# Two cross-attention blocks on one core: fp16 parts for the projections of x and context, a buffer for the gate, another head and another order

## The reference

```
block 0 (8 heads of 40):
  hs   = attention(x Wq, enc Wk, enc Wv)        enc = context[:, :124]   (FIRST)
  q1   = ca^T Wq_ca, 128 of its 192 rows        ca  = context[:, 124:]   (4 tokens)
  hs1  = attention(q1, x, x)                                             (CA)
  hs2  = attention(hs1 Wq, ca Wk_ca, ca Wv_ca)
  x    = (hs + hs2) Wout + b_out + x
block 1 (20 heads of 16):
  h = ln1(x); x = attention(h q1, h k1, h v1) o1_w + o1_b + x            (SELF)
  h = ln2(x); x = attention(h q2, context k2, context v2) o2_w + o2_b + x  (CROSS)
  h = ln3(x); a, g = split(h ff_w1 + ff_b1); x = (a * gelu(g)) ff_w2 + ff_b2 + x
```

## Time and profile before

| what | value |
|---|---|
| runs | 3941.24, 3950.0, 3958.27 us, median 3950.0 |
| profiled execution | 3965.49 us, its span 3963.6 us |
| granted TensorE clock, mean | 0.966 |
| PE / PEld / DVE / ACT / POOL busy | 90% / 72% / 58% / 57% / 50% |

### The profile page before, as it was taken

The page is one execution under the profiler, slowest core; times in us unless marked ns, Lnnn a source line. Parts: engine busy times, 40 slices in busy tenths (PEclk is TensorE's granted clock), DMA queues, the critical chain, the costliest instruction groups (busy, mean ns, idle before and its releaser), DMA issues.

```text
span 3963.6 us, 112057 instructions
## 1 busy us (share of the span) xinstructions
PE 3580.9 (90%) x38314; PEld 2867.6 (72%) x38314; DVE 2308.9 (58%) x5535; ACT 2268.7 (57%) x4084; POOL 1966.4 (50%) x2229
## 2 busy tenths in 40 slices
PE   6499999999999999999999999999999999999999
PEld 5377777777777777777777777777777777777777
DVE  6466556556555655655556556555655656556555
ACT  2356655665556556556655665566566556655664
POOL 0345444554555445555554554545445555554553
PEclk9799999999999999999999999999999999999999
DMA  4332333222233332232333322233332232333321
GB/s 138 63 61 53 58 61 66 59 46 60 59 55 61 67 61 49 53 65 51 63 63 66 59 46 60 56 58 61 67 64 47 53 64 53 63 63 66 59 46 42
DMA packets 417600, 238.71 MB, mean 60 GB/s; under 512 B 44315, under 2 KB 416715, under 8 KB 416843
## 3 DMA queue, kind: packets, MB, share of 16 engines
q1 hardware_dynamic: 405317, 229.62, 29.6%
q10 hardware_dynamic: 11910, 3.04, 0.3%
HBM read 153.50 MB, written 79.06 MB: 59 GB/s over the span
## 4 chain that ended last, share of the span: by engine, by line
PE 36%; issue 30%; POOL 17%; DVE 5%; SPq 4%; DMA 3%; ACT 3%; POOLq 1%; ACTq 0%; DVEq 0%
PE bank L1412 35%; POOL PT L519 10%; DMA xin<-in_x 3%; DVE mx L1025 2%; ACT PT L742 2%; POOL cQ L526 2%; POOL XA L496 1%; POOL cK L526 1%; SPq L365 1%; POOL rstd L566 1%; SPq L363 1%; POOL XB L496 1%; PE bank L1446 1%; PE bank L1531 1%; SPq L361 1%
## 5 line engine op out<-in xcount | busy, mean ns | idle before, releaser
L519 POOL TENSOR_TENSOR PT<-P,PT 128x512 f16<-128x512 f32 (+1 forms) x924 | 1068.8, 1157 | 642.1 <-ACT PT L742 640.8
L1412 PE MATMUL bank<-hT,w_ff_w 128*128 128x256 f16 x5440 | 651.6, 277 | 1.7 <-DVE hT L1054 1.7
L1025 DVE TENSOR_REDUCE mx<-bank 128x4 f32<-128x512 f32 (+1 forms) x924 | 579.6, 680 | 104.4 <-PE bank L1412 96.5
L1412 PEld LDWEIGHTS bank<-hT,w_ff_w 128*128 128x128 f16 x5440 | 532.5, 100 | 73.2 <-issue 6.5
L1412 PE MATMUL bank<-mxs,pick 84*128 84x128 f16 (+1 forms) x3696 | 513.4, 220 | 0.0
L1412 PE MATMUL bank<-w_ff,F 128*128 128x320 f32 x1360 | 411.5, 442 | 1.3 <-DVE F L1104 1.3
L1412 PEld LDWEIGHTS bank<-mxs,pick 84*128 84x128 f16 (+1 forms) x3696 | 375.1, 103 | 16.8 <-issue 8.2
L1412 PEld LDWEIGHTS bank<-V,PT 128*128 128x128 f16 (+1 forms) x9504 | 314.5, 96 | 84.0 <-POOL PT L519 37.9
L723 ACT ACTIVATE P<-bank,ff_b,scale 128x256 f32<-128x256 f32 x340 | 187.8, 562 | 324.9 <-PE bank L1412 285.4
L1412 PE MATMUL bank<-Qs,Ks 96*128 96x128 f16 x2640 | 361.7, 220 | 0.1
L1412 PE MATMUL bank<-V,PT 128*128 128x17 f16 (+1 forms) x9504 | 343.7, 172 | 17.1 <-POOL PT L519 14.3
(11 more groups left out here) (274 smaller groups left out, 7295.4 us busy)
## 6 DMA issues: line engine op xcount, KB each, us to landing
Ks<-scratch_k SPq DMA_DIRECT2D x198, 160.0 KB, 4.5
Qs<-scratch_q SPq DMA_DIRECT2D x198, 160.0 KB, 5.7
scratch_k<-cK SPq DMA_DIRECT2D x134, 128.0 KB, 1.8
scratch_q<-cQ SPq DMA_DIRECT2D x134, 128.0 KB, 2.1
Q0s<-scratch_q SPq DMA_DIRECT2D x99, 160.0 KB
K0s<-scratch_k SPq DMA_DIRECT2D x99, 160.0 KB
cT<-in_cT SPq DMA_DIRECT2D x136, 96.0 KB, 2.0
xin<-in_x SPq DMA_DIRECT2D x34, 320.0 KB, 3.2
```

The source lines that it names most:

```text
L519: nc.gpsimd.tensor_tensor(PT[0:keys, n % PT_SLOTS, 1, :], P[0:keys, n % P_SLOTS, :], PT[0:keys, n % PT_SLOTS, 0, :], ALU.subtract).then_in ...
L1025: nc.vector.tensor_reduce(mx[:, g % 2, 4 * u:4 * u + 4], bank[:, :].rearrange("p (h s) -> p h s", h=4)[:, :, 0:keys], axis=AX.X, op=ALU.ma ...
L1412: return nc.tensor.matmul(o, lhsT, rhs, start=start, stop=stop)
```

## The change

Inputs x and context are scaled by a power of two and split into fp16 parts once a step (`split_x` and `split_context` on ACT, three activations each; `low_x` and `low_context` on POOL), and `Wq`, `Wk`, `Wv`, `k2`, `v2` become fp16 parts in the head. `Q0T` is then 8 fp16 matmuls a chunk and `K0T`, `K2T`, `V0`, `V2` are 5 each. `gate` becomes a tile of its own, and the waits between `gelu` and `exps` go. The high and low chunks use `fixed` factors. `V2` and `K2T` read the same context parts as `V0` and `K0T`, so `cT2` and its loads go. `load_next` comes right after `stack_self` on SP and waits for `vca` and for the context's low part. The order of all engines is another one: `ff0` to `ff3` stand among the first scores, `ff4` to `ff9` as before between SELF and CROSS; `K0T0` to `K0T2` come together early; `K2T0`, `K2T1` and `V0_1` before CROSS. In the head the products of the tokens come first, in four parts with a store each, the shifts are spread beside the splitting, the reduces take the absolute value in one pass, and POOL does most of the clearing.

```diff
+MATSX, MATSK = ("Wq",), ("Wk", "Wv", "k2", "v2")
+MATS16 = MATSN + MATSX + MATSK
+PASSES_C = ((1, 0, 0), (3, 0, 0), (1, 1, 0), (2, 0, 1), (2, 1, 1))
+PASSES_X = ((1, 0, 0), (1, 1, 0), (4, 0, 0), (2, 0, 1), (2, 1, 1), (5, 0, 1), (3, 0, 2), (3, 1, 2))
...
-    Q0T0 XT0_0 Q0T1 XT0_1 Q0T2 K1T0 K1T1 K1T2 Q1T0 Q1T1 Q1T2 S0 S1 V0_0 V1_0 mx0 S2 S3 T0 K0T0 T1
-    V1_1 mx1 K0T1 T2 S4 S5 S6 S7 S8 T3 vca mx2 S9 S10 T4 S11 S12 T5 S13 caT0 T6 mx3 T7 T8 caT1 K0T2
-    T9 T10 T11 T12 T13 V0_1 outT1_0 ff0 ff1 outM1_0 outT1_1 ff2 ff3 outM1_1 XT1_0 ff4 s4 XT1_1 ff5
-    Q2T0 Q2T1 Q2T2 ff6 ff7 mT ff8 mB ff9 S14 S15 S16 S17 y1 S18 S19 mx4 S20 S21 S22 T14 S23 K2T0 T15
...
+    Q0T0 XT0_0 XT0_1 S0 Q0T1 Q0T2 K1T0 K1T1 K1T2 Q1T0 Q1T1 Q1T2 S1 ff0 S2 S3 ff1 ff2 mx0 K0T0 ff3 T0
+    V1_0 K0T1 mx1 K0T2 V0_0 T1 V1_1 T2 S4 S5 S6 S7 S8 T3 vca mx2 S9 T4 S10 T5 S11 T6 S12 S13 caT0
+    mx3 T7 T8 T9 T10 T11 T12 T13 caT1 ff4 outT1_0 ff5 ff6 ff7 outT1_1 outM1_0 outM1_1 ff8 XT1_0 ff9
+    XT1_1 s4 Q2T0 Q2T1 Q2T2 mT mB V0_1 K2T0 K2T1 y1 S14 S15 S16 S17 S18 mx4 S19 S20 T14 S21 T15 S22
...
-        gate = P[:, 0, :].rearrange("p (t n) -> p t n", t=2)
+        gate = sb("gate", [128, 2, GS])
...
             def load_next(i):
-                sp.wait_ge(v_done, v_job(i, LOOP_JOBS, "V0_1"))
+                sp.wait_ge(v_done, v_job(i, LOOP_JOBS, "vca"))
+                sp.wait_ge(c16_ready, i + 1)
...
+            def low_x(i):
+                pool.wait_ge(x_high, i + 2)
+                nc.gpsimd.tensor_tensor(x16[:, 3:6, :], xT[:, :, :], x16[:, 0:3, :], ALU.subtract).then_inc(x16_ready, 1)
+            def low_context(i):
+                pool.wait_ge(c_high, i + 1)
+                nc.gpsimd.tensor_tensor(c16[:, 2:4, :], cT[:, :, :], c16[:, 0:2, :], ALU.subtract).then_inc(c16_ready, 1)
...
+            def split_x(i):
+                act.wait_ge(step_loaded, i * LOADS_STEP + 2 * LOADS_STEP)
+                act.wait_ge(next_ready, i + 2)
+                act.wait_ge(j_full, done(i, LOOP_JOBS.number("Q0T2"), "J"))
+                nc.scalar.activation(xT[:, :, :], xT[:, :, :], ACT.Copy, scale=next_factor[:, SX:SX + 1])\
+                    .then_inc(x_scaled, 1)
+                act.wait_ge(x_scaled, i + 2)
+                nc.scalar.activation(x16[:, 0, :], xT[:, 0, :], ACT.Copy, scale=lower[:, :])
+                nc.scalar.activation(x16[:, 1:3, :], xT[:, 1:3, :], ACT.Copy).then_inc(x_high, 1)
...
-                elif t == 0:
-                    act.wait_ge(low_p, units_done(min(i, STEPS) if isinstance(i, int) else i, LAST_UNIT[SELF, 1]))
+                else:
+                    act.wait_ge(v_done, v_job(i - 1, LOOP_JOBS, f"ff{FFT + t - 2}"))
...
-                if n == LAST_UNIT[SELF, 1] + 1:
-                    act.wait_ge(v_done, v_job(i, LOOP_JOBS, f"ff{FFT - 1}"))
...
-            def chunk(i, name, c, wn, rows_k, src, at, rows):
-                if name == "K2T":
-                    pe.wait_ge(step_loaded, i * LOADS_STEP + 2 * LOADS_STEP)
+            def chunk(i, name, c, wn, src, passes, at, rows):
+                if c == 0:
+                    pe.wait_ge(x16_ready if src is x16 else c16_ready, i + 1)
                 bank = j_next(i, LOOP_JOBS, f"{name}{c}")
-                transposed(bank, wn, rows_k, src, at[c], rows[c]).then_inc(j_full, 1)
+                transposed16(bank[0:rows[c], 0:GS], wn, src, at[c], rows[c], passes).then_inc(j_full, 1)
...
             pe.wait_ge(tokens_loaded, TOKENS)
...
+            row_shifts_of(1, "q1")
             pe.wait_ge(kca_copied, 1)
+            products(0)
+            products(1)
+            row_shifts_of(0, "k1")
+            row_shifts_of(3, "v1")
+            products(2)
+            row_shifts_of(2, "q2").then_inc(row_shifts, 1)
+            products(3)
...
+            ff_shifts(0, 6)
...
             extremes_turned(-1, HEAD_JOBS)
+            ff_shifts(6, 13)
             extremes_everywhere(-1, HEAD_JOBS, QUANTITIES)
+            ff_shifts(13, 2 * FFT).then_inc(shifts_ready, 1)
```

More of the change, by code:

```diff
@@ L583, in _ @@
             token_queries(-1)
+            low_x(-1)
             assert links[0] == POOL_HEAD_LINKS
@@ L1173, in _ @@
                                         None, ALU.mult)
-            for m, n in enumerate(MATSN):
+            link(-1, nc.vector.memset(amax[:, :, :], 0.0))
+            dve.wait_ge(kca_ready, 1)
+            for c, r in enumerate(CH0):
+                for h in range(HC0[c]):
+                    last = nc.vector.tensor_scalar(
+                        kca[c][0:r, :, h, :], j_bank[c + 2][0:r, 0:B * T4].rearrange("p (b t) -> p b t", t=T4),
+                        mask0[0:r, h:h + 1], None, ALU.mult)
@@ new lines, in _, with lows @@
+            link(-1, last)
+            link(-1, nc.vector.tensor_scalar(qk_b[:, :], qk_b[:, :], scale[:, 2:3], None, ALU.mult))
+            extremes(128, 9, qk_b[:, :], AX.X)
+            dve.wait_ge(scale_ready, 1)
+            highs = [0]
+            def lows(names):
+                for n in names:
+                    for k in range(BLOCKS[n]):
+                        highs[0] += 1
+                        dve.wait_ge(high_ready, highs[0])
+                        last = nc.vector.scalar_tensor_tensor(out=w16[n][:, 1, k, :], in0=raw[n][:, k, :],
+                                                              scalar=gains[:, NORM_OF[n], k:k + 1], in1=w16[n][:, 0, k, :],
+                                                              op0=ALU.mult, op1=ALU.subtract)
+                return last
@@ L1469, in chunk16, with values @@
                 transposed16(bank[0:CH1[c], 0:GS], wn, hTn, AT1[c], CH1[c]).then_inc(j_full, 1)
-            def values(i, name, b, wn, src):
+            def values(i, name, b, wn):
+                if b == 0:
+                    pe.wait_ge(c16_ready, i + 1)
                 bank = j_next(i, LOOP_JOBS, f"{name}_{b}")
-                for k, rk in enumerate(CHC):
-                    last = mm(bank[:, 0:H], src[0:rk, k, b * S:(b + 1) * S], w[wn][0:rk, k, :], k == 0, k == 1)
+                for x, (blk, part, rows) in enumerate(PASSES_C):
+                    last = mm(bank[:, 0:H], c16[:, blk, b * S:(b + 1) * S], w16[wn][:, part, rows, :],
+                              x == 0, x == len(PASSES_C) - 1)
                 last.then_inc(j_full, 1)
@@ L1845, in _ @@
-                shares4(i)
-                exponents(i, 24)
-                attend(i, 22)
-                turn_maxima(i, 7)
-                exponents(i, 25)
-                out_proj(i, 2, 0)
-                chunk(i, "K2T", 1, "k2", CHC, cT2, AT1, CH1)
+                attend(i, 22)
+                exponents(i, 25)
+                ff_part(i, 0, 8, 10)
                 attend(i, 23)
                 exponents(i, 26)
-                attend4(i, 0)
+                out_proj(i, 2, 0)
+                values(i, "V2", 0, "v2")
```

695 lines of the change are left out of this document (362 added, 333 removed).

## The result

The changed kernel takes 3789.1 us (3782.3 to 3797.1) against 3950.0: ratio 0.9594, 95% interval 0.9564 to 0.9623. It is faster by 4.1% where 7.6% was forecast. The time lies in the stated range (3560 to 3810), but outside the band that stands for the forecast itself (3570 to 3740), and it is 27 us from rival (1) and 139 from the forecast. The profiled execution takes 3797.1 us, 168.4 less than that of before.

What follows compares the result with a forecast made beforehand. The prediction took PE's work, with waits from its order, to bound a pass, and serial steps the head: 33 x (6.0 + 1.7) = 254 plus 51 is 305 off 3965.5, 3660, so about 3650 us; range 3560 to 3810.

Steps and rivals of the forecast that it cites:

- rival (1): Chains through POOL, ACT and DRAM show as waits: a pass only 2 to 3 us shorter, 3816 us; chance 0.17.
- a pass is set by what PE has to do: In each pass, PE's work (busy 105.5 of 114.5 us), 9 us of true idle and waits from its order set the time.
- 33 x 6.0 = 198: Projections of x and context in fp16 instead of fp32: 6.0 us less in each of 33 passes.
- the 1.4 of my own text: K1T begins about 1.4 us earlier by the cheaper Q0T; nothing taken for the context's split, with this among the reasons.
- The order and the gate: Early ff0 to ff3 fill PE's waits at CA, less losses at the chain and tables: 1.7 us a pass won.
- The idle time at `attend`: PE's wait for POOL's low part at the CA units, 2.8 us a pass, which the early ff jobs can fill.
- The loss of 2: Between SELF and CROSS, with 7 us of ff gone, the chain has less to hide behind: some 2 us a pass lost.
- The tables: Two more ACT table switches a pass at 1.28 us each, some of 2.6 lost; by the skill's page 2.8 more.
- The splits: Splitting x and context on ACT (3.4 us plus 0.3) and POOL (1.2 and 1.7): nothing taken; bound 2.9 a pass.
- SP's: load_next with its ten DMAs goes ahead of K0T0's put on SP and waits for vca: no cost.
- The head: Before the first Wq matmul: splitting and biases end at 86, matmul at about 101 us instead of 152.1, 51 less.
- (3): ACT becomes the bound in CA and SELF: 10 us a pass lost against 7.7 won, 3975 us, slower; chance 0.06.

Runs made afterwards that it cites:

- cut_before: The kernel before, with the fp32 products of Wk, k2, Wv and v2 over the first 96 channels alone: 4001.0 us, ratio to before 1.0148.
- none_early: The changed kernel with no feed-forward job ahead of the CA units, all ten between SELF and CROSS: 4004.5 us, ratio 1.0175.
- no_switch: The changed kernel with Identity in place of Gelu in ff0 to ff3, so two table switches a pass fewer: 3828.5 us, ratio 0.9694.
- cut_after: The changed kernel without the passes that use a low part in the projections of x and context: 3849.3 us, ratio 0.9739.

## Why the prediction was right in sign and wrong in size

**Luck first.** The sign was right, and the time is inside the stated range. But the range reaches 70 us above the forecast's own band, and the measured time lies there, by a mechanism that the prediction gave 0.17.

**The step that failed** is "a pass is set by what PE has to do", with the waits beside it taken as they were, and with it the term 33 x 6.0 = 198. The work itself went as forecast, 6.4 a pass off by busy time. But links of the pass are round trips through DRAM, ScalarE's `Exp` units, and VectorE in the turn, and only matmuls ahead of a link's start or longer than the link count. All of the change together took 3.85 off a pass, where the projections alone had 6.0. Of that 1.5 stand ahead of `K1T` (the 1.4 of my own text, 3 x 1.46 against 3 x 0.97, which I set off against the context's split), 1.3 ahead of `Q2T`, and 1.4 in the turn; the link from `K1T` to S4 gave 0.9 back. cut_before shows it of the kernel before too: 3.2 us a pass less of busy time were worth 1.0 at the same clock in SELF, and nothing with the clock as it fell. That PE was busy for 90% was no bound. How the 3.85 divide into projections, gate and order, no run shows.

**The order and the gate (+1.7 a pass, bounds 5 and -4).** The idle time at `attend` went, 2.8 a pass as forecast. The early jobs alone are worth 5.5 a pass with the rest as changed, by none_early. This is above the bound of 5 for gate and order together, and it can't be added to a price of the projections: none_early takes 116.1 a pass against 114.5 before, with 7 us more of it at the lower clock, and 3.8 of it stand in the link to S14, where it has more jobs than before. The new projections in the old order, which would settle it, were not tried. The loss of 2 forecast for the chain from SELF to CROSS did not come: 1.3 less up to `Q2T`, and 13.4 for 13.6 from there.

**The tables (bound 2.6 a pass).** CA's first `Exp` is 4.2 later, with four loads a pass of 1.28, and it costs next to nothing, since S4 waits for the DMA anyway: two loads less are worth 0.4 at most, by the passes of no_switch at the full clock. **The splits** cost nothing, as taken: there is no wait for x16 or c16, and the last load of Q is issued 12.2 us after `K1T` began, 12.3 before. **SP's** part is less sure: this load lands 9.0 us after its issue, 8.0 before, which is the 0.9 given back, and what makes it slower no run shows.

**The head (51).** 43 came. The term that was mis-sized is the end of splitting and biases, 94.7 for 86; POOL's part behind it was right, and the stores of the tokens did not matter.

**The clock** was in none of the steps. The changed kernel spends 7.5 us a pass at half clock against 6.7; taking that away is worth 1.1 a pass, some 25 us by the runs. In the runs with less work for PE it grew, and hid part of what they won.

**The rivals.** (1), waits take the place of the matmuls, had the mechanism, and 2.5 a pass where 3.85 came; the time is 27 us from its 3816. (3), ACT as the bound in CA and SELF, did not come: SELF's last `Exp` is at 44.6, before at 45.4. What would show the forecast wrong was named well: PE's idle time before CROSS's `Ks,Qs` (0.39 in the row above) stayed under 3 and SELF's first `Exp` came at 30.6, not behind 31, but passes of 106 to 108 did not come.

What stays open: 0.6 of the 1.5 that cut_after's turn lost; why the clock falls in SELF in 14 of cut_before's passes and 17 of no_switch's, and in 4 of the changed kernel's; and what the gate's buffer alone and the new projections alone are worth, which wasn't tried.

## What to carry to other kernels

When one engine is busy for 90%, check before pricing its work that this is not filling put under waits: take a part of that work out and look whether the time moves, and compare passes at the same granted clock, since less work can bring more time at the lower one. Cut the pass into links at the waits that end in a DMA or another engine, and price an edit by the link that it lies in; work that only covers a round trip is worth nothing until it is longer than the trip, and taking it away leaves room that must be filled by moving other work in. And look at the granted clock of each stretch before and after: here 2.3 us of idle time ahead of a dense stretch cost 1.1 more behind it, and filling it with useless work was a gain.
